# Attention scores of a head pair in one burst, the maxima moved to SBUF, and corner transposes two at a time

## The chip, the cores and the metric

The kernel runs on one core of one Trainium2 chip. The time is the device time of one execution, in microseconds (us); lower is better. The kernel before took 3621.35 us, the median of 3 runs (3619.87 to 3623.71). PE is TensorE, DVE is VectorE, ACT is ScalarE, POOL is GpSimd; SP issues the DMAs here.

## The reference, cut to what matters

The input x has 16 sequences of 256 tokens and 128 channels. It is normalised, and the result goes through a selective scan (the first 330 us or so of the kernel, not touched by the change) and through a stack of six layers of local attention and a gated feed-forward part; the two are multiplied at the end. The change is in the attention:

```
for i in range(DEPTH):                                   # 6
    x = attn_layer(shift_tokens(x), Wqkv[i], ...) + x
    x = ffn_layer(shift_tokens(x), ln_g[i], ...) + x

# attn_layer: 16 heads of 64, windows of 32
qkv = x @ Wqkv;  q, k = l2norm and rotary of q, k
sim = einsum('bhwie,bhwje->bhwij', bq, bk2) * QK_SCALE   # a query sees its own window and the one before
sim = where(mask, -max, sim);  attn = softmax(sim)
out = einsum('bhwij,bhwje->bhwie', attn, bv2);  return out @ Wo
```

## The kernel before, in words

The 4096 tokens are 8 groups of two sequences (512 columns). One group in one layer is an item; there are 48. `flow` runs `turn` once per item on every engine, and the turns of four items overlap: `turn` has the roles prev2, prev, cur and nxt. A turn has 16 steps, and a step is one (head pair p, sequence b) with p = s // 2 and b = s % 2. All order is written out by hand; the engines are tied by semaphores alone. A wait of an engine holds up all that is behind it on that engine.

In step s of a turn PE does, in this order: `scores(s)` (line 844, eight 64x64 matmul tiles of 96 columns for head pair p and sequence b, the two heads of the pair into banks 0 and 1); what `bank_work` gives for "dn", "wo", "rqT" and "cen" together with `down` and `project_out` (lines 911, 883, 789, 889); on even steps `outputs` (line 872, 16 products of probabilities and values); `transpose_probs` of three steps ago (lines 853 and 854, into bank 2); on odd steps a piece of v (lines 355 to 357 with 256 columns); then `bank_work` for "qk", the feed-forward products and the variance (lines 355 to 357 with 512 columns, and 893), and every fourth step `square_sums` (line 826).

DVE does `denominators` (a reciprocal, line 1633), `copy_probs` (line 1639 transposes two 32x32 corners in SBUF, line 1640 copies bank 2), `products` (two rotary products of qk block s - 1, line 1608), and `maxima(s)`: four masked copies of the scores with a running maximum (line 1653, each followed by the read of its accumulator), and one multiplication of the four maxima by the scale of the head (line 1659, `nb`). The four maxima, `mx`, lie in four columns of bank 1 in PSUM. `scores(s)` waits for `sc_bias` of step s - 1, which line 1659 sets, since both use the same columns of banks 0 and 1. ACT then takes the exponentials (`probabilities`, line 1181), and copies v and the outputs out of bank 3 (lines 1195 and 1190). POOL normalises the probabilities (line 1343, after the reciprocal), adds the halves of the rotary product (`rotate`, line 1357, after a DMA has swapped partitions) and scales k (`scale_k`, line 1363, in some steps); in steps 10 to 13 it also has the layer norm and the low parts (lines 1373, 1375, 1386, 1381).

Of the kernel before, what the change touches and what calls it, by code (L numbers as in the profile page):

```python
# [123 lines left out]
SCORE_TILES = [(0, 0, 0), (1, 32, 32), (2, P, P - WINDOW), (3, P + 64, P + 32)]  # L124
# [11 lines left out]
def build(nc, x_in, W_in, W_xdbl, W_dt, W_out, mvec, Wqkv, Wo, W1, W2, lvec, tabs_c, mask_c, ident_c,  # L136
          headsum_c, conv_w, out):
    ctx = ExitStack()
    with ctx:
        def sb(name, shape, dt=F32):  # L140
            return ctx.enter_context(nc.sbuf_tensor(name, shape, dt))
# [48 lines left out]
        nb = sb("nb", [P, STEPS, 2, 2])  # L190
        den = sb("den", [P, STEPS, 2, 2])
# [13 lines left out]
        mx = bank[1][:, UW:UW + 4].rearrange("p (t i) -> p t i", t=2)  # L205
# [142 lines left out]
        def head_scale(t, p, b):  # L348

            m = p % 4 // 2  # L350
            return t[:, p // 4, 2 * b:2 * b + 2, p % 2, 2 * m:2 * m + 2]
# [240 lines left out]
        def _(pe):  # L592
# [167 lines left out]
            def turn(n, o, par, gs, kind, l):  # L760
# [70 lines left out]
                def scores(s):  # L831

                    p, b = s // 2, s % 2
                    scaled = (n8 + (p + 1))
                    used = (n16 + s)
                    if b == 0:
                        pe.wait_ge(k_norm, scaled)
                    pe.wait_ge(sc_bias, used)
                    c0 = b * SEQ
                    for half, c, k0 in SCORE_TILES:  # L840
                        part = slice(64 * (half % 2), 64 * (half % 2) + 64)
                        for i in range(2):
                            rows = slice(64 * i, 64 * i + 64)
                            mm = pe.matmul(bank[i][part, c:c + 96], rot[rows, p, c0 + 64 * half:c0 + 64 * half + 64],  # L844
                                           rot[rows, PAIRS + p, c0 + k0:c0 + k0 + 96], start=True, stop=True)
                    mm.then_inc(sc_ps, 1)
# [107 lines left out]
                for s in range(16):  # L954
# [5 lines left out]
                    if cur is not None:  # L960
                        scores(s)
# [9 lines left out]
                    if s % 2 == 0 and s < 6 and prev is not None:  # L971
                        outputs(s, s // 2 + 5, prev)
                    if s % 2 == 0 and s >= 6 and cur is not None:
                        outputs(s, s // 2 - 3, cur)
# [447 lines left out]
        def _(dve):  # L1422
# [164 lines left out]
            def turn(n, o, par, gs, kind, l):  # L1587
# [47 lines left out]
                def copy_probs(e, q):  # L1635
# [3 lines left out]
                    dve.transpose(pt[96:128, e % 4, :, 0, P:P + WINDOW], pr[0:32, e % 4, :, 1, 0:WINDOW])  # L1639
# [3 lines left out]
                def maxima(s):  # L1643

                    p, b = s // 2, s % 2
                    scores = (n16 + (s + 1))
                    used = (n16 + (s - 1 if s >= 2 or prev is not None else 0))
                    dve.wait_ge(sc_ps, scores)
# [165 lines left out]
```

## Time and profile before

| what | value |
|---|---|
| runs | 3619.87, 3621.35, 3623.71 us; median 3621.35 us |
| profiled execution: its own time, its span | it is given by its span alone: 3621.6 us, 95570 instructions |
| PE | 3397.7 us busy, 94% |
| DVE | 3201.4 us busy, 88% |
| ACT | 3008.5 us busy, 83% |
| POOL | 2872.2 us busy, 79% |
| granted clock of PE | 0.9 to 1.0 of full speed in every slice |

How to read it: the share of busy time is a mean, and matmuls are pipelined with modelled ends, so that 94% of PE is not PE at its peak. The chain of waits tells which engine was the last to arrive at each place. In the rows further down, a row of the timeline is: start in us, duration in us, engine, line, operation, written tile and read tiles, their shapes, how many, and in brackets the idle time before it and what ended it. A row of the chain is: start, length on the chain, and what it was.

### The profile page before, as it was taken

What the parts mean: (1) busy time and instruction counts of PE and PEld (TensorE: products, weight loads), DVE (VectorE), ACT (ScalarE), POOL (GpSimd) and SP (SyncE); (2) the same over time, 40 slices, a digit from 0 to 9 for tenths busy, and PEclk for the clock granted to TensorE, in tenths of its full rate; (3) what the DMA queues carried; (4) which work ended last, traced back from release to release, by engine and by line L of the source; (5) the groups of instructions that cost most, each with busy time, mean ns of one, the idle gap of its engine ahead of it and who ended that gap; (6) DMA issues with size and microseconds to landing.
All of it is one profiled execution on the core that took longest, in us unless ns stands there. A gap on an engine that the chain in (4) does not pass through costs nothing.

```text
span 3621.6 us, 95570 instructions
## 1 busy us (share of the span) xinstructions
PE 3397.7 (94%) x30862; PEld 2172.1 (60%) x30862; DVE 3201.4 (88%) x11640; ACT 3008.5 (83%) x8812; POOL 2872.2 (79%) x2383
## 2 busy tenths in 40 slices
PE   7887999999999999999999999999999999999998
PEld 3444666666666666666666666666666666666665
DVE  6997988988888988998988988988988988998997
ACT  6554888888888888888888888888888888888887
POOL 6887887887887887887788887888787788887783
PEclk9998999999999999999999999999999999999999
DMA  5443322333322333323332332333332333332322
GB/s 160 141 133 121 111 101 101 107 113 106 112 102 100 106 115 103 116 101 100 107 115 103 113 106 96 109 118 102 114 103 98 104 120 105 111 106 98 104 103 92
DMA packets 261741, 396.41 MB, mean 109 GB/s; under 512 B 45566, under 2 KB 86588, under 8 KB 261244
## 3 DMA queue, kind: packets, MB, share of 16 engines
q1 hardware_dynamic: 261244, 390.30, 32.1%
q8 instruction: 249, 4.08, 0.5%
q14 instruction: 248, 2.03, 0.2%
HBM read 157.91 MB, written 6.03 MB: 45 GB/s over the span
## 4 chain that ended last, share of the span: by engine, by line
PE 51%; DVE 22%; POOL 10%; issue 9%; ACT 6%; DMA 1%; SPq 1%; DVEq 0%; POOLq 0%; ACTq 0%
PE bank L883 8%; DVE ab L1608 6%; PE bank L872 6%; PE bank L844 5%; PE bank L355 5%; PE bank L357 5%; PE bank L356 5%; PE bank L826 4%; DVE sm L1653 4%; PE bank L911 4%; PE bank L853 3%; POOL rot L1357 3%; DVE wide L1500 3%; POOL pr L1343 3%; PE bank L854 2%
## 5 line engine op out<-in xcount | busy, mean ns | idle before, releaser
L1181 ACT ACTIVATE pr<-sm,nb,rq 128x128 f32<-128x128 f32 (+1 forms) x3072 | 1517.4, 501 | 16.4 <-DVE nb L1659 16.0
L1343 POOL TENSOR_TENSOR pr<-pr,rden 128x640 f32<-128x640 f32 x768 | 963.6, 1255 | 494.6 <-DVE rden L1633 493.6
L1608 DVE TENSOR_TENSOR ab<-bank,ltab 128x512 f32<-128x512 f32 x1520 | 974.3, 683 | 78.9 <-PE bank L357 64.9
L1357 POOL TENSOR_TENSOR rot<-ab,swp 128x512 f32<-128x512 f32 x760 | 974.6, 1282 | 83.2 <-DMA swp<-ab 82.2
L1653 DVE CUSTOM_DVE_ANT_0 sm<-bank,mask 128x128 f32<-128x128 f32 (+1 forms) x3072 | 841.0, 330 | 43.2 <-PE bank L844 42.4
L1181 ACT ACTIVATION_READ_ACCUMULATOR pr<-sm,nb,rq 128x1 f32 x3072 | 596.6, 194 | 0.0
L844 PEld LDWEIGHTS bank<-rot 64*64 64x64 f32 x12288 | 288.3, 132 | 440.2 <-issue 341.2
L1640 DVE COPY pt<-bank 128x512 f32<-128x512 f32 x768 | 531.4, 692 | 10.2
L1363 POOL TENSOR_TENSOR rot<-rot,rkb 128x512 f32<-128x512 f32 x384 | 490.3, 1282 | 52.6 <-DMA rkb<-k_scratch 51.9
L1169 ACT ACTIVATE sq<-bank 128x512 f32<-128x512 f32 x768 | 452.4, 589 | 62.4 <-DVE ab L1608 49.5
L844 PE MATMUL bank<-rot 64*64 64x96 f32 x12288 | 432.1, 256 | 64.0 <-POOL rot L1363 34.1
L872 PEld LDWEIGHTS bank<-pt,vtok 128*64 128x64 f32 x6144 | 369.2, 137 | 197.7 <-issue 144.2
L872 PE MATMUL bank<-pt,vtok 128*64 128x160 f32 (+1 forms) x6144 | 462.2, 293 | 27.1 <-ACT vtok L1195 27.1
L1653 DVE DVE_READ_ACCUMULATOR2_ANT bank<- 128x1 f32 x3072 | 437.2, 142 | 0.0
L853 PE MATMUL bank<-ident,pr 128*128 128x128 f32 x1536 | 409.1, 293 | 17.8 <-DVE pt L1640 17.5
L1195 ACT ACTIVATE vtok<-bank 128x512 f32<-128x512 f32 x384 | 228.0, 594 | 220.2 <-PE bank L357 220.2
L854 PE MATMUL bank<-ident,pr 128*128 128x128 f32 x1536 | 377.6, 273 | 0.0
L883 PE MATMUL bank<-wide,wo 128*128 128x512 f32 x768 | 370.9, 606 | 0.0
L1190 ACT ACTIVATE wide<-bank 128x512 f32<-128x512 f32 x384 | 227.6, 593 | 156.7 <-PE bank L872 156.2
L355 PE MATMUL bank<-xh,wqk_h 128*128 128x512 f32 x768 | 335.6, 437 | 10.3 <-ACT sq L1169 7.0
L1639 DVE STREAM_TRANSPOSE pt<-pr 32x64 f32<-32x64 f32 x768 | 183.1, 238 | 158.2 <-PE bank L854 137.9
L357 PE MATMUL bank<-xl,wqk_h 128*128 128x512 f32 x768 | 305.5, 398 | 0.0
(213 smaller groups left out, 6160.6 us busy)
## 6 DMA issues: line engine op xcount, KB each, us to landing
swp<-ab SPq DMA_DIRECT2D x1520, 128.0 KB, 2.0
rkb<-k_scratch SPq DMA_DIRECT2D x768, 128.0 KB, 2.9
rot<-c_scratch SPq DMA_DIRECT2D x64, 256.0 KB, 3.3
sq<-c_scratch SPq DMA_DIRECT2D x64, 256.0 KB, 3.2
xs<-xT SPq DMA_DIRECT2D x95, 128.0 KB, 2.3
xs<-xT SPq DMA_DIRECT2D x95, 127.5 KB, 2.4
raw<-Wqkv SPq DMA_DIRECT2D x48, 128.0 KB, 2.5
wo<-Wo SPq DMA_DIRECT2D x6, 512.0 KB, 4.8
```

The source lines that it names most:

```text
L355: eng.matmul(o, wh, ah, start=True, stop=False)
L844: mm = pe.matmul(bank[i][part, c:c + 96], rot[rows, p, c0 + 64 * half:c0 + 64 * half + 64], rot[rows, PAIRS + p, c0 + k0:c0 + k0 + 96], st ...
L853: pe.transpose(bank[2][:, 256 * i:256 * i + P], pr[:, e % 4, i, 0, 0:P], ident[:, :])
L872: mm = pe.matmul(bank[3][64 * i:64 * i + 64, cols], vtok[:, 2 * b + t, ch], pt[:, e % 4, i, t, 0:cols.stop - cols.start], start=(b == 0 an ...
L883: mm = pe.matmul(use_bank("wo", 0)[:, :], wo[:, p, :], wide[:, p, :], start=(p == 0), stop=(p == PAIRS - 1))
L1181: ins = act.activation(pr[:, s % 4, i, t, 0:P + WINDOW * t], sm[:, s % 2, i, cs], ACT.Exp, bias=nb[:, s, t, i:i + 1], scale=head_scale(rq, ...
L1343: ins = pool.tensor_tensor(pr[:, e % 4, :, :, :], pr[:, e % 4, :, :, :], rden[:, e, :, :].rearrange("p t i -> p i t").unsqueeze(3) .to_bro ...
L1357: pool.tensor_tensor(rot[:, PAIRS * (j % 2) + j // 2, :], ab_of(j, 0, lead), swp_of(j, lead), ALU.add).then_inc(qk_rot, 1)
L1363: pool.tensor_tensor(rot[:, PAIRS + p, :], rot[:, PAIRS + p, :], rkb[:, p % KSLOT, :], ALU.mult)\
L1608: ins = dve.tensor_tensor(seqs(ab_of(j, i, lead)), seqs(qk_bank(j, lead)[:, :]), ltab[:, 2 * (j % 2) + i:2 * (j % 2) + i + 1, :] .to_broad ...
L1640: dve.tensor_copy(pt[:, e % 4, :, :, 0:P], bank[2][:, :].rearrange("p (i t c) -> p i t c", i=2, t=2)).then_inc(p_Tsb, 1)
L1653: ins = dve.tensor_tensor_reduce(sm[:, s % 2, i, cs], bank[i][:, cs], mask[:, cs], 1.0, -3e38, ALU.add, ALU.max, mx[:, t, i:i + 1])
```

## The change

Six things change. (1) PE's `scores` runs on even steps only and does both sequences of the head pair in one burst of 16 tiles; it waits for `nb` of the two steps before, once. (2) In banks 0 and 1 the scores of the two sequences now lie side by side (256 columns each), at the column of their key; the first tile has 64 columns in place of 96. DVE's `maxima` reads them there, and waits for the burst, which on odd steps has long been there. (3) With the banks full, `mx` moves from bank 1 to an SBUF tile, one set of four for each sequence. (4) PE's `outputs` stands right behind the scores, ahead of "dn", "wo", "rqT" and "cen". (5) `copy_probs` transposes the corners of steps e and e + 1 in one instruction at even e, and none at odd e; that one also waits for POOL's `p_norm` of e + 1. (6) Semaphore counts follow.

```diff
-SCORE_TILES = [(0, 0, 0), (1, 32, 32), (2, P, P - WINDOW), (3, P + 64, P + 32)]
+SCORE_TILES = [(0, 64), (32, 96), (P - WINDOW, 96), (P + 32, 96)]
+        mx = sb("mx", [P, 2, 2, 2])
-        mx = bank[1][:, UW:UW + 4].rearrange("p (t i) -> p t i", t=2)
@@ PE
-                def scores(s):
-                    p, b = s // 2, s % 2
-                    scaled = (n8 + (p + 1))
-                    used = (n16 + s)
-                    if b == 0:
-                        pe.wait_ge(k_norm, scaled)
-                    pe.wait_ge(sc_bias, used)
-                    c0 = b * SEQ
-                    for half, c, k0 in SCORE_TILES:
-                        part = slice(64 * (half % 2), 64 * (half % 2) + 64)
-                        for i in range(2):
-                            rows = slice(64 * i, 64 * i + 64)
-                            mm = pe.matmul(bank[i][part, c:c + 96], rot[rows, p, c0 + 64 * half:c0 + 64 * half + 64],
-                                           rot[rows, PAIRS + p, c0 + k0:c0 + k0 + 96], start=True, stop=True)
+                def scores(p):
+                    pe.wait_ge(k_norm, n8 + (p + 1))
+                    pe.wait_ge(sc_bias, n16 + 2 * p)
+                    for b in range(GB):
+                        c0 = b * SEQ
+                        for m, (k0, count) in enumerate(SCORE_TILES):
+                            part = slice(64 * (m % 2), 64 * (m % 2) + 64)
+                            for i in range(2):
+                                rows = slice(64 * i, 64 * i + 64)
+                                mm = pe.matmul(bank[i][part, c0 + k0:c0 + k0 + count],
+                                               rot[rows, p, c0 + 64 * m:c0 + 64 * m + 64],
+                                               rot[rows, PAIRS + p, c0 + k0:c0 + k0 + count], start=True, stop=True)
                     mm.then_inc(sc_ps, 1)
...
-                    if cur is not None:
-                        scores(s)
+                    if s % 2 == 0 and cur is not None:
+                        scores(s // 2)
+                    if s % 2 == 0 and s < 6 and prev is not None:
+                        outputs(s, s // 2 + 5, prev)
+                    if s % 2 == 0 and s >= 6 and cur is not None:
+                        outputs(s, s // 2 - 3, cur)
                     bank_work(s, ("dn", "wo", "rqT", "cen"))
...
-                    if s % 2 == 0 and s < 6 and prev is not None:
-                        outputs(s, s // 2 + 5, prev)
-                    if s % 2 == 0 and s >= 6 and cur is not None:
-                        outputs(s, s // 2 - 3, cur)
@@ DVE
-                    dve.transpose(pt[96:128, e % 4, :, 0, P:P + WINDOW], pr[0:32, e % 4, :, 1, 0:WINDOW])
+                    if e % 2 == 0:
+                        both = slice(e % 4, e % 4 + 2)
+                        dve.wait_ge(p_norm, n16 + (16 * q + e + 2))
+                        dve.transpose(pt[96:128, both, :, 0, P:P + WINDOW], pr[0:32, both, :, 1, 0:WINDOW])
...
-                    dve.wait_ge(sc_ps, scores)
+                    dve.wait_ge(sc_ps, n8 + (p + 1))
...
-                            ins = dve.tensor_tensor_reduce(sm[:, s % 2, i, cs], bank[i][:, cs], mask[:, cs],
-                                                           1.0, -3e38, ALU.add, ALU.max, mx[:, t, i:i + 1])
+                            keys = slice(b * SEQ, b * SEQ + P) if t == 0 else slice(b * SEQ + P - WINDOW, b * SEQ + SEQ)
+                            ins = dve.tensor_tensor_reduce(sm[:, s % 2, i, cs], bank[i][:, keys], mask[:, cs],
+                                                           1.0, -3e38, ALU.add, ALU.max, mx[:, b, t, i:i + 1])
...
-                    dve.tensor_tensor(nb[:, s, :, :], mx, head_scale(nrq, p, b), ALU.mult).then_inc(sc_bias, 1)
+                    dve.tensor_tensor(nb[:, s, :, :], mx[:, b, :, :], head_scale(nrq, p, b), ALU.mult).then_inc(sc_bias, 1)
```

PE at steps 0 and 1 of a turn, before: `rot` are the rotated q and k (scores), `gg,w` is the down product, `pt,vtok` the outputs, `ident,pr` the transposes.

```order
L844 MATMUL bank<-rot 64x96 x8
L911 MATMUL bank<-gg,w 128x512
L872 MATMUL bank<-pt,vtok 64x160 x2
L872 MATMUL bank<-pt,vtok 64x128 x2
L872 MATMUL bank<-pt,vtok 64x160 x2
L872 MATMUL bank<-pt,vtok 64x128 x2
L853 MATMUL bank<-ident,pr 128x128
...
L826 MATMUL bank<-sq,headsum 32x512 x4
L844 MATMUL bank<-rot 64x96 x8
L911 MATMUL bank<-gg,w 128x512
L853 MATMUL bank<-ident,pr 128x128
```

The same place of PE in the changed kernel:

```order
L841 MATMUL bank<-rot 64x64 x2
L841 MATMUL bank<-rot 64x96 x6
L841 MATMUL bank<-rot 64x64 x2
L841 MATMUL bank<-rot 64x96 x6
L870 MATMUL bank<-pt,vtok 64x160 x2
L870 MATMUL bank<-pt,vtok 64x128 x2
L870 MATMUL bank<-pt,vtok 64x160 x2
L870 MATMUL bank<-pt,vtok 64x128 x2
L909 MATMUL bank<-gg,w 128x512
...
L826 MATMUL bank<-sq,headsum 32x512 x4
L909 MATMUL bank<-gg,w 128x512
L851 MATMUL bank<-ident,pr 128x128
```

The second burst has joined the first, and the outputs have moved ahead of the down product.

DVE at the end of a step and the start of the next, before (every step reads so); `mask` rows are the maxima, `ISA bank 128x1` the read of an accumulator, and the waits are in brackets:

```order
L1653 ISA sm,bank<-bank,mask 128x160
L1653 ISA bank 128x1
L1659 TENSOR_TENSOR nb<-bank,nrq 128x4 [waits sc_max]
L1633 RECIPROCAL rden<-den 128x4 [waits p_exp]
L1639 STREAM_TRANSPOSE pt<-pr 32x2x32 [waits o_ps,p_T]
L1640 COPY pt<-bank 128x4x128
L1608 TENSOR_TENSOR ab<-bank,ltab 128x512 [waits qk_rot,qk_proj]
```

DVE in the changed kernel, at the start of an even step and then of an odd one:

```order
L1654 ISA mx 128x1
L1660 TENSOR_TENSOR nb<-mx,nrq 128x4 [waits sc_max]
L1631 RECIPROCAL rden<-den 128x4 [waits p_exp]
L1640 STREAM_TRANSPOSE pt<-pr 32x4x32 [waits p_norm,o_ps,p_T]
L1641 COPY pt<-bank 128x4x128
...
L1654 ISA mx 128x1
L1660 TENSOR_TENSOR nb<-mx,nrq 128x4 [waits sc_max]
L1631 RECIPROCAL rden<-den 128x4 [waits p_exp]
L1641 COPY pt<-bank 128x4x128 [waits o_ps,p_T]
```

One transpose in two steps is gone, and both inputs of the multiplication that makes `nb` now lie in SBUF, where one of them lay in PSUM.

## Rows read from the trace of the kernel before

**Rows 1.** The page, parts 1 and 4: busy time, and the chain by engine.

```profile
PE 3397.7 (94%) x30862; PEld 2172.1 (60%) x30862; DVE 3201.4 (88%) x11640; ACT 3008.5 (83%) x8812; POOL 2872.2 (79%) x2383
PE 51%; DVE 22%; POOL 10%; issue 9%; ACT 6%; DMA 1%; SPq 1%; DVEq 0%; POOLq 0%; ACTq 0%
```

**Rows 2.** The chain, 1500 to 1640 us: start, length, what.

```profile
1522.99 1.06 PE bank L889 x2
...
1561.05 0.49 PE bank L844 x16
1561.54 1.06 PE bank L911 x2
...
1564.94 1.91 PE bank L883 x4
1566.86 1.13 PE bank L872 x16
1567.99 0.26 PE bank L853
...
1570.82 1.72 PE bank L883 x4
1572.54 0.11 PE bank L853
...
1584.36 1.13 PE bank L872 x16
...
1590.76 1.06 PE bank L889 x2
```

**Rows 3.** Timeline of PE inside one burst of scores.

```profile
2011.31 0.31 PE L844 MATMUL bank<-rot 64*64 64x96 f32 x4
...
2011.31 0.56 PE L844 MATMUL bank<-rot 64*64 64x96 f32 x16
```

**Rows 4.** Timeline of DVE and ACT from step 5 to step 9 of a turn.

```profile
1578.96 0.24 DVE L1639 STREAM_TRANSPOSE pt<-pr 32x64 f32<-32x64 f32 x1 [1.68 <-PE bank L854]
...
1586.34 0.16 DVE L1659 TENSOR_TENSOR nb<-bank,nrq 128x4 f32<-128x4 f32 x1
...
1586.62 0.24 DVE L1639 STREAM_TRANSPOSE pt<-pr 32x64 f32<-32x64 f32 x1
1586.87 0.69 DVE L1640 COPY pt<-bank 128x512 f32<-128x512 f32 x1
...
1589.87 0.16 DVE L1659 TENSOR_TENSOR nb<-bank,nrq 128x4 f32<-128x4 f32 x1
...
1592.06 0.58 ACT L1255 ACTIVATE gg<-bank 128x512 f32<-128x512 f32 x1
...
1596.15 0.69 DVE L1666 TENSOR_SCALAR rsum<-bank 128x512 f32<-128x512 f32 x1 [0.33 <-PE bank L826]
```

**Rows 5.** The page, part 5: the rotary products on DVE.

```profile
L1608 DVE TENSOR_TENSOR ab<-bank,ltab 128x512 f32<-128x512 f32 x1520 | 974.3, 683 | 78.9 <-PE bank L357 64.9
```

**Rows 6.** Line 1448 of the prologue: its eight instructions, durations in ns.

```profile
L1448 DVE TENSOR_TENSOR rsum<-rsum x8: 135/136/734, 7.4 to 215.2; 128x4 f32<-128x4 f32 x8
```

**Rows 7.** Timeline of DVE and POOL around two of these eight.

```profile
40.74 1.27 POOL L1310 TENSOR_TENSOR wide<-wide,rot 128x512 f32<-128x512 f32 x1
41.29 0.73 DVE L1448 TENSOR_TENSOR rsum<-rsum 128x4 f32<-128x4 f32 x1
...
111.82 0.14 DVE L1448 TENSOR_TENSOR rsum<-rsum 128x4 f32<-128x4 f32 x1
111.98 1.27 POOL L1310 TENSOR_TENSOR wide<-wide,sq 128x512 f32<-128x512 f32 x1 [1.31 <-DVE wide L1500]
```

**Rows 8.** Timeline of POOL and DVE, steps 7 and 14 of the same turn.

```profile
1589.61 1.29 POOL L1363 TENSOR_TENSOR rot<-rot,rkb 128x512 f32<-128x512 f32 x1
...
1615.65 1.30 POOL L1357 TENSOR_TENSOR rot<-ab,swp 128x512 f32<-128x512 f32 x1
...
1615.84 0.16 DVE L1659 TENSOR_TENSOR nb<-bank,nrq 128x4 f32<-128x4 f32 x1
```

More of the change, by code:

```diff
@@ L1645, in maxima @@
                     p, b = s // 2, s % 2
-                    scores = (n16 + (s + 1))
                     used = (n16 + (s - 1 if s >= 2 or prev is not None else 0))
-                    dve.wait_ge(sc_ps, scores)
+                    dve.wait_ge(sc_ps, n8 + (p + 1))
                     dve.wait_ge(p_exp, used)
```

## The prediction, made before the changed kernel was run

> **What bounds the kernel now.** I read the page first, then the chain of waits over two items, then the timelines of DVE, PE and POOL in the stretches that the chain names. On the page two engines are nearly full, and the chain goes through PE for half of the span and through DVE for a fifth [rows 1]; so the question is where each of the two is last. The chain answers it. The centring product of step 8 starts at 1522.99 and again at 1590.76: an item takes 67.77 us [rows 2], and 48 of them make 3253 of the 3621.6 us. Inside an item there are two stretches. The PE stretch runs from the feed-forward products of step 14 to the transposes of step 4: every piece of the chain there is a PE piece behind a PE piece (1561.05 to 1572.54 show a part) [rows 2]. The DVE stretch begins at step 5, where DVE waits 1.68 us for those transposes, and then has no idle time from 1578.96 until step 9, where it waits 0.33 us for the square sums at 1596.15 [rows 4]; behind that it goes on without idle time to the rotary products of step 14, whose square lets ACT load the table of gelu, on which the next PE stretch waits. PE and DVE are close to each other at step 8, but a gain on PE between steps 5 and 13 buys nothing by itself.
>
> The page's execution has a span of 3621.6 us and the median of the runs is 3621.35 us, so the sum is made against the span and carries over as it is.
>
> **PE, bursts.** On the chain a burst costs 0.49 us, and then the first full-array product behind it costs more than without it: two passes of the down product take 1.06 us behind a burst, and four of the output projection 1.91 against 1.72; the first transpose 0.26 behind a tiled product and 0.11 behind a full one [rows 2]. So an odd step without its burst saves 0.49 + about 0.17 = 0.66 us. The even step's burst doubles: four passes end 0.31 us after its start and sixteen 0.56 [rows 3], which is 0.083 for two tiles of 96 columns; eight tiles more are 0.33, and two pairs of 64 columns in place of 96 give back 0.028 each, so +0.27. Had the longer burst the full price again it would be +0.49; I keep 0.27, since nothing new starts inside it. A pair of steps saves 0.39.
>
> **PE, outputs ahead of the rest.** They cost 1.13 both behind a full product (1566.86) and right behind scores (1584.36) [rows 2]. One pass between tiled and full array goes away on steps 0, 2, 4 and 8: 0.15 each (0.26 less 0.11). What they wait for is there already: the copy of bank 2 that they need precedes, on DVE, the `nb` for which the scores have just waited.
>
> **The sum of the PE stretch.** Three bursts go (steps 15, 1, 3): 3 x 0.66 = 1.98. Three grow: 3 x 0.27 = 0.81. Three reorderings: 0.45. Gain 1.6 us an item. DVE stays ahead of it here: it works 3.5 us a step [rows 4], where the mean step of an item is 67.77 / 16 = 4.2 and the steps of this stretch are longer than the mean.
>
> **DVE, corners.** Today a step of DVE is 3.53 us from one `nb` to the next (1586.34 to 1589.87), of which the corner transpose takes 0.25 (1586.62 to 1586.87) [rows 4]. An odd step loses these 0.25. On an even step 64 columns become 128: at the slope of the rotary product, 683 ns for 512 columns [rows 5], that is +0.085; bounds are 0 and +0.24. In steps 5 to 14, up to the products of step 14: 5 x 0.25 - 5 x 0.08 = 0.85. About 0.15 is lost again at step 9, since PE reaches the square sums for which DVE waits only behind the scores, outputs, centring and variance of step 8, 0.12 later than now. 0.7 stays. The added wait for `p_norm` of e + 1 costs nothing: POOL's normalisation begins right behind the reciprocal of the step before and takes 1.3 us, while the transpose comes 3.5 us later; queued behind it are the copy of bank 2 and all of the step.
>
> **DVE, `mx` in SBUF.** This is the part with a price that the diff doesn't show. `nb` becomes a product of two SBUF inputs. No instruction of the layers is one now, but the prologue has one of the same size: line 1448, 128 x 4 elements, both inputs and output in SBUF. Of its eight, the median takes 136 ns and one 734 [rows 6]. The one of 734 ns starts at 41.29 while a POOL product is under way (40.74 to 42.01) and ends at 42.02 with it; one of 136 starts at 111.82, when POOL idles [rows 7]. So it waits for the POOL instruction under way, and frees itself about 0.11 us before what the subtraction says (0.60 us late at a remainder of 0.72).
>
> The Trainium skill, "SBUF — State Buffer", section "Who interferes with whom", says that a DVE instruction with two SBUF inputs contends with a GpSimd instruction that reads SBUF, because its second input comes through the shared read interface, and that one with a single SBUF input does not. By that rule `nb` starts to wait, and the maxima, the reciprocal and the corners do not; all POOL instructions here read SBUF. The trace agrees in the one case that it has. Without the rule and that case the sum would be that of the first rival, 3532 us.
>
> How often: I laid every `nb` of the trace beside POOL's instruction under way. In the turn of rows 8, seven of the ten `nb` of steps 5 to 14 fall into one; the first of these is at step 7, 1589.87 in 1589.61 to 1590.90, 1.03 us before its end, the last at step 14, 1615.84 in 1615.65 to 1616.95, 1.11 [rows 4, 8]. Over all 48 items steps 5 to 13, those that lie ahead of the products of step 14, have 4.2 us of such remainders an item (step 12 and 13 0.85 and 0.94 each, step 7 0.69, steps 5, 6 and 8 hardly any); the PE stretch has 0.9, of which PE sees nothing. With 0.11 off each of some seven hits that is 3.4. That is the upper end if nothing moves. But each wait leaves DVE just behind an end of POOL's, and POOL (79% busy) itself waits for DVE's reciprocal, so the hits thin out. Stepping through the turn of rows 4 and 8 with DVE steps of 3.29 and 3.61 us, I find waits at steps 7, 9, 10, 11 and 13 and none at 8 and 12. The lower end is the average of steps 12 and 13 and a trifle, 1.9. I take 2.9, nearer to the row-by-row reading than to that, less the 0.7 of the corners: the DVE stretch gets 2.2 us longer an item. The accumulator reads that now write SBUF, four a step at 142 ns, are taken at no change; nothing shows them either way, and 10 ns each would be 0.3 us an item.
>
> **Sum.** 2.2 - 1.6 = +0.6 us an item; of 48 items the first and the last have half of each: 47 x 0.6 = 28 us. 3621.6 + 28 = 3650 us.
>
> **Rivals.**
> - *The small product doesn't wait.* For: seven of the eight of line 1448 took 136 ns. Against: at those seven POOL was idle. Then the gain of the PE stretch, 1.6, and of DVE's corners in steps 5 to 8, 0.4, stand; ACT gives back 0.1: it copies the centred sums right after its exponentials (at 1592.06 [rows 4]), these come 1.4 us later now that burst and outputs are in front, and its copy of v is then late for the outputs of step 10. 1.9 x 47 = 89 us: 3532 us.
> - *The hits don't thin out, and the PE stretch feels them too.* For: POOL has more work than DVE in steps 9 to 13, so an `nb` there nearly always finds it busy. Loss 3.4 in the DVE stretch less 0.7, plus 0.3 where `nb` of step 1 or 3 now holds up the next burst, against a gain of 1.2 where the burst has its full price: +1.8 x 47 = 85 us, 3706 us, and 3735 where POOL's weight splits come on top.
> - *The waits are absorbed.* They come to 1.9, a loss of 1.2 in the DVE stretch net of the corners; gain 1.6: -0.4 x 47 = -19 us, 3603 us; it decides at a wait of 2.3 us an item, where the gain of 1.6 and the 0.7 are used up. Below that the kernel is faster than before: this is the other side of the forecast.
> - *It doesn't save the switches*: the 0.17 behind a burst belongs to whatever comes first in a step. Then the three odd steps save 0.49 only and the gain is 1.1: +1.1 x 47 = 52 us, 3673 us; it lies in the forecast's own range.
>
> **How the numbers follow.** Forecast with the last rival, 3625 to 3690: 0.47. Full hits, 3690 to 3740: 0.13. Absorbed, 3560 to 3625: 0.25. No wait, about 3532: 0.15. A measurement of this kernel tells a change of 0.2%, 7 us, from none: 3614 to 3629. About 0.05 of the forecast and 0.04 of the absorbed case lie there, so faster 0.36, same 0.09, slower 0.55. The range that leaves out the no-wait case and the ends of the others is 3550 to 3725; the forecast's own is 3625 to 3690.
>
> **What would show it.** `nb` should grow from 162 ns to a mean of 300 to 500, with single ones up to 1.3 us, and each long one should end with a POOL instruction; if it stays near 150 ns, the first rival holds. The matmul bursts should be 384 with about 0.76 us on the chain, followed by outputs at 1.13, and the odd steps should start with a transpose of 0.11 or a projection at 1.72 for four. The corners should be 384 of 0.3 us. The item should take about 68.4 us, DVE's share of the chain should rise and PE's fall below 50%. The prediction is wrong in its larger part if the item stays under 67.4 us.

## The result, and the profile after

| kernel | median, us | lowest to highest | runs |
|---|---|---|---|
| before | 3621.35 | 3619.74 to 3623.71 | 5 |
| after | 3633.72 | 3631.35 to 3637.96 | 5 |

The changed kernel takes 1.0034 of the time before, 95% interval [1.0023, 1.0045]: 12.4 us slower, where +28 was forecast.

The page of the changed kernel, parts 1 and 4, against [rows 1]:

```profile
span 3632.4 us, 95188 instructions
...
PE 3315.3 (91%) x30862; PEld 2180.4 (60%) x30862; DVE 3202.3 (88%) x11256; ACT 3016.2 (83%) x8812; POOL 2882.2 (79%) x2383
...
PE 44%; DVE 25%; ACT 16%; issue 10%; POOL 4%; DMA 1%; DVEq 0%; SPq 0%; ACTq 0%; POOLq 0%
```

PE is busy for 82 us less, and its products of the scores (lines 844 and 841) for 88 us less: 343.6 in place of 432.1. DVE is as busy as before, though half of the corner transposes are gone. ACT's share of the chain went from 6 to 16%: nothing in the forecast spoke of that. The clock has no part in the difference: its mean over the span is 0.995 of full speed in both kernels. (The table before the change says 0.9 or more for every slice; in both kernels the fourth of the 40 slices, around the end of the scan, shows 0.8 to 0.9.)

DVE's groups that the change touches, before and then after: line, engine, operation, written and read tile, shapes, count, then busy us and mean ns of one, then idle time before them.

```profile
L1653 DVE CUSTOM_DVE_ANT_0 sm<-bank,mask 128x128 f32<-128x128 f32 (+1 forms) x3072 | 841.0, 330 | 43.2 <-PE bank L844 42.4
...
L1653 DVE DVE_READ_ACCUMULATOR2_ANT bank<- 128x1 f32 x3072 | 437.2, 142 | 0.0
...
L1639 DVE STREAM_TRANSPOSE pt<-pr 32x64 f32<-32x64 f32 x768 | 183.1, 238 | 158.2 <-PE bank L854 137.9 <-issue 0.6
...
L1659 DVE TENSOR_TENSOR nb<-bank,nrq 128x4 f32<-128x4 f32 x768 | 124.5, 162 | 26.2
```

```profile
L1654 DVE CUSTOM_DVE_ANT_0 sm<-bank,mask 128x128 f32<-128x128 f32 (+1 forms) x3072 | 753.6, 301 | 4.3 <-PE bank L841 4.2
...
L1660 DVE TENSOR_TENSOR nb<-mx,nrq 128x4 f32<-128x4 f32 x768 | 332.8, 433 | 26.6
...
L1654 DVE DVE_READ_ACCUMULATOR2_ANT mx<- 128x1 f32 x3072 | 253.8, 83 | 0.0
...
L1640 DVE STREAM_TRANSPOSE pt<-pr 32x128 f32<-32x128 f32 x384 | 116.9, 304 | 13.7 <-PE bank L852 1.5 <-issue 0.3
```

`nb` grew from 162 to 433 ns, inside the 300 to 500 that was asked for. The corners are 384 of 304 ns, as priced. But the reads of the accumulator fell from 142 to 83 ns and the masked copies from 330 to 301, which was priced at nothing. Part of a copy's record lies under its read; by their starts in the timelines the four copies and reads of a step take 1.02 us where they took 1.20.

Timeline of DVE and POOL in the changed kernel, two `nb` with the POOL instructions that run beside them:

```profile
1592.44 1.27 POOL L1355 TENSOR_TENSOR rot<-ab,swp 128x512 f32<-128x512 f32 x1
...
1593.38 0.35 DVE L1660 TENSOR_TENSOR nb<-mx,nrq 128x4 f32<-128x4 f32 x1
...
1601.32 1.28 POOL L1371 TENSOR_TENSOR gg<-gg 128x512 f32<-128x512 f32 x1
...
1601.97 0.65 DVE L1660 TENSOR_TENSOR nb<-mx,nrq 128x4 f32<-128x4 f32 x1
```

The first ends at 1593.73, POOL's rotation at 1593.71; the second ends at 1602.62 and POOL's product at 1602.60. So it is in the whole trace: 406 of the 768 `nb` take more than 0.22 us, and each of them ends within 0.03 us of the end of a POOL instruction. The wait is the one forecast from line 1448 [rows 6, 7].

The chain of the changed kernel, from the table of gelu to step 3, which answers to [rows 2]:

```profile
1553.72 0.60 ACT wide L1188
1554.32 1.61 ACT pr L1179 x7
...
1556.28 0.49 ACT sq L1167
1556.81 0.50 PE bank L355
...
1557.78 0.82 PE bank L841 x29
1558.60 1.13 PE bank L870 x16
...
1561.92 1.00 PE bank L826 x8
1562.91 1.06 PE bank L909 x2
...
1567.77 1.91 PE bank L881 x4
...
1570.82 0.86 PE bank L909 x2
1571.68 1.72 PE bank L881 x4
```

Three things are to be seen. A double burst costs 0.82 us, 0.33 more than the single one and not 0.27 (some of its 32 records are missing). At step 3 the switch is saved in full: the down product takes 0.86 and four passes of the projection 1.72. At step 1 it isn't: the down product still takes 1.06, now behind the square sums of line 826. And the chain enters the PE stretch through ACT: block 15 of q and k (line 355 at 1556.81) starts only when ACT has squared block 14, which stands behind all exponentials of step 14.

The waits that the change made or took away; the first fence is the kernel before, the second the changed one. Who waited, for whom, us in total, times, longest.

```profile
ACT wide L1190 <- PE bank L872: 156.2, 137, 1.6
...
PEld bank L355 <- ACT sq L1169: 42.9, 141, 2.1
...
ACT pr L1181 <- DVE nb L1659: 16.0, 52, 5.0
...
DVE rsum L1666 <- PE bank L826: 15.5, 46, 0.4
...
PE bank L355 <- ACT sq L1169: 7.0, 6, 1.9
...
DVE rq L1617 <- PE bank L789: 1.3, 2, 0.8
```

```profile
ACT pr L1179 <- DVE nb L1660: 156.6, 195, 6.0
...
PEld bank L355 <- ACT sq L1167: 71.3, 129, 4.0
...
DVE rq L1615 <- PE bank L789: 61.0, 48, 2.2
...
ACT gg L1253 <- PE bank L887: 53.9, 47, 1.2
...
DVE rsum L1667 <- PE bank L826: 40.7, 47, 0.9
...
PE bank L355 <- ACT sq L1167: 23.4, 59, 3.8
```

ACT no longer waits for the outputs. In exchange DVE waits for the product rqT, ACT for the centring product (both stand behind the outputs now), PE longer for ACT's square, and ACT longer for `nb`.

To place the time I took the end of each of the 768 `nb` and summed the time from one to the next over two parts of the item, as means of items 3 to 46, in us. The same was done for the runs of the next section:

| kernel | steps 6 to 13 | steps 14 to 5 | item |
|---|---|---|---|
| before | 30.48 | 37.71 | 68.19 |
| after | 31.49 | 36.90 | 68.39 |
| b1, before with `mx` in SBUF | 32.15 | 37.57 | 69.72 |
| b3, the same with the lock taken away | 30.19 | 37.53 | 67.72 |
| a1, after with the lock taken away | 29.98 | 36.84 | 66.82 |
| a2, after with rqT and cen first | 31.06 | 37.04 | 68.10 |
| e1, a2 with the square moved | 31.00 | 36.55 | 67.55 |

So DVE's stretch lost 1.0 and PE's won 0.8. "The lock" below is `nb`'s wait for POOL's instruction. In a1, b3, c2, d3 and f1 `nb` is made from four columns of scores in place of the maxima, so that one input is in PSUM; the maxima are made and written all the same, but `nb` leaves them out, and so these five kernels do not compute the reference.

### The profile page after: what moved, and what is told of

Same layout as the page of the kernel before. It is cut to its first block, busy times and chain, and to the rows that moved or that the text cites. A ratio compares the mean times of both kernels' runs of the same rounds, so it can differ in the third digit from the quotient of the medians.

```text
span 3632.4 us, 95188 instructions
## 1 busy us (share of the span) xinstructions
PE 3315.3 (91%) x30862; PEld 2180.4 (60%) x30862; DVE 3202.3 (88%) x11256; ACT 3016.2 (83%) x8812; POOL 2882.2 (79%) x2383
## 4 chain that ended last, share of the span: by engine, by line
PE 44%; DVE 25%; ACT 16%; issue 10%; POOL 4%; DMA 1%; DVEq 0%; SPq 0%; ACTq 0%; POOLq 0%
PE bank L881 8%; DVE ab L1606 8%; PE bank L870 7%; ACT pr L1179 6%; DVE sm L1654 6%; PE bank L841 5%; PE bank L909 4%; PE bank L355 4%; PE bank L357 3%; PE bank L356 3%; DVE wide L1498 3%; DVE pt L1641 3%; PE bank L826 2%; PE bank L851 2%; PE bank L852 2%
## 5 line engine op out<-in xcount | busy, mean ns | idle before, releaser
L1606 DVE TENSOR_TENSOR ab<-bank,ltab 128x512 f32<-128x512 f32 x1520 | 974.9, 683 | 43.8 <-PE bank L357 35.9
L1654 DVE CUSTOM_DVE_ANT_0 sm<-bank,mask 128x128 f32<-128x128 f32 (+1 forms) x3072 | 753.6, 301 | 4.3 <-PE bank L841 4.2
L1641 DVE COPY pt<-bank 128x512 f32<-128x512 f32 x768 | 525.4, 684 | 95.3 <-PE bank L852 86.8
L1167 ACT ACTIVATE sq<-bank 128x512 f32<-128x512 f32 x768 | 454.9, 592 | 86.7 <-DVE ab L1606 79.6
L870 PE MATMUL bank<-pt,vtok 128*64 128x160 f32 (+1 forms) x6144 | 461.4, 292 | 41.0 <-ACT vtok L1193 38.8
L851 PE MATMUL bank<-ident,pr 128*128 128x128 f32 x1536 | 399.2, 287 | 38.3 <-DVE pt L1641 38.3
L841 PE MATMUL bank<-rot 64*64 64x96 f32 (+1 forms) x12288 | 343.6, 243 | 86.7 <-DVE nb L1660 77.1
L841 PEld LDWEIGHTS bank<-rot 64*64 64x64 f32 x12288 | 275.7, 133 | 233.6 <-issue 147.7
L851 PEld LDWEIGHTS bank<-ident,pr 128*128 128x128 f32 x1536 | 215.0, 140 | 299.3 <-issue 254.9
L852 PE MATMUL bank<-ident,pr 128*128 128x128 f32 x1536 | 377.8, 273 | 0.0
L1660 DVE TENSOR_TENSOR nb<-mx,nrq 128x4 f32<-128x4 f32 x768 | 332.8, 433 | 26.6
L356 PE MATMUL bank<-xh,wqk_l 128*128 128x512 f32 x768 | 302.7, 394 | 0.0
```

The costliest lines, as they stand in the source:

```text
L841: mm = pe.matmul(bank[i][part, c0 + k0:c0 + k0 + count], rot[rows, p, c0 + 64 * m:c0 + 64 * m + 64], rot[rows, PAIRS + p, c0 + k0:c0 + k0 ...
L851: pe.transpose(bank[2][:, 256 * i:256 * i + P], pr[:, e % 4, i, 0, 0:P], ident[:, :])
L870: mm = pe.matmul(bank[3][64 * i:64 * i + 64, cols], vtok[:, 2 * b + t, ch], pt[:, e % 4, i, t, 0:cols.stop - cols.start], start=(b == 0 an ...
L1606: ins = dve.tensor_tensor(seqs(ab_of(j, i, lead)), seqs(qk_bank(j, lead)[:, :]), ltab[:, 2 * (j % 2) + i:2 * (j % 2) + i + 1, :] .to_broad ...
L1641: dve.tensor_copy(pt[:, e % 4, :, :, 0:P], bank[2][:, :].rearrange("p (i t c) -> p i t c", i=2, t=2)).then_inc(p_Tsb, 1)
L1654: ins = dve.tensor_tensor_reduce(sm[:, s % 2, i, cs], bank[i][:, keys], mask[:, cs], 1.0, -3e38, ALU.add, ALU.max, mx[:, b, t, i:i + 1])
```

## The experiments

Each ran beside the kernel before, whose median was 3620.42 to 3623.37 us there; ratios are against it, with 95% intervals.

| run | median, us | ratio |
|---|---|---|
| a1_psum_operand | 3553.36 | 0.9815 [0.9801, 0.9828] |
| b1_mx_sbuf | 3689.15 | 1.0187 [1.0173, 1.0201] |
| b3_mx_sbuf_psum_operand | 3598.33 | 0.9938 [0.9924, 0.9952] |
| b2_corners_pair | 3607.40 | 0.9965 [0.9952, 0.9977] |
| a3_outputs_old | 3627.33 | 1.0019 [1.0010, 1.0028] |
| a2_rq_cen_first | 3616.59 | 0.9988 [0.9979, 0.9997] |
| c1_four_scalars | 3642.53 | 1.0058 [1.0045, 1.0070] |
| c2_psum_rq_cen | 3547.83 | 0.9797 [0.9783, 0.9810] |
| f1_psum_single | 3564.08 | 0.9838 [0.9825, 0.9852] |
| d1_nb_on_pool | 3717.76 | 1.0264 [1.0250, 1.0278] |
| d2_nb_pool_square | 3700.06 | 1.0217 [1.0199, 1.0234] |
| d3_psum_square | 3525.34 | 0.9732 [0.9719, 0.9746] |
| e1_a2_square | 3593.53 | 0.9921 [0.9907, 0.9934] |
| e3_before_square | 3619.38 | 0.9992 [0.9983, 1.0001] |
| e2_b2_square | 3605.99 | 0.9958 [0.9945, 0.9972] |

**a1, the changed kernel without the lock.**

```diff
-dve.tensor_tensor(nb[:, s, :, :], mx[:, b, :, :], head_scale(nrq, p, b), ALU.mult).then_inc(sc_bias, 1)
+near = bank[1][:, 0:4].rearrange("p (t i) -> p t i", t=2)
+dve.tensor_tensor(nb[:, s, :, :], near, head_scale(nrq, p, b), ALU.is_lt).then_inc(sc_bias, 1)
```

> The changed kernel, but the product that makes nb reads four columns of bank 1 (PSUM) in place of mx and only compares them with the scale, so the maxima are not used and its output is not the reference's; instructions, counts and waits are the same, mx is still written to SBUF. Theory (the port wait): nb falls from a mean of 433 ns to about 165, no long ones are left, the stretch of DVE from step 5 to 13 loses its 3.2 us of waits an item; since PE and ACT are close behind, some 2 to 2.5 us of it reach the item: 3633.7 - 47 x 2.25 = about 3528 us (3515 to 3545). Rival (the waits are hidden behind ACT or PE, and the small gain of the change is all that there is): 3615 us or more.

Measured: 3553.36 us, 80 less than the changed kernel, where 89 to 119 less were expected. The chain on its page, and the group of `nb`:

```profile
PE 48%; ACT 32%; DVE 7%; issue 6%; POOL 5%; DMA 1%; SPq 0%; DVEq 0%; ACTq 0%; POOLq 0%
...
L1661 DVE TENSOR_TENSOR nb<-bank,nrq 128x4 f32<-128x4 f32 x768 | 124.1, 162 | 26.7
```

`nb` is back at 162 ns, with the same size and the same tiles around it. The lock is shown, and its price here: without it the change would be faster than before. But it costs 80 us for 3.15 us of waits an item (what the `nb` of steps 5 to 13 take over 0.15 us each), which would be 148 over 47 items. The rest was hidden behind other waits of DVE, which come out when the lock is taken away:

```profile
DVE pt L1641 <- PE bank L852: 139.6, 236, 2.4
DVE ab L1606 <- PE bank L357: 97.7, 220, 1.9
...
DVE rden L1631 <- ACT pr L1179: 75.3, 100, 1.3
```

In the changed kernel these three were 86.8, 35.9 and 43.0 us; together they grow by 147 us. The chain says who is next: ACT has 32% of it.

**b1 and b3, the lock and the reads in the kernel before.** b1 moves `mx` to SBUF and does nothing else; b3 adds a1's edit to b1.

```diff
+        mx = sb("mx", [P, 2, 2])
-        mx = bank[1][:, UW:UW + 4].rearrange("p (t i) -> p t i", t=2)
...
```

> The kernel before with mx in an SBUF tile and nothing else changed. Both theories expect accumulator reads of 83 ns in place of 142 and 1.02 us in place of 1.20 from the first maximum to nb, and nb at 350 to 500 ns. Theory (waits outweigh the faster reads): nine steps save 0.18 each = 1.6 us, waits of about 3.2 us come, so +1.6 x 47 = 75 us, less what moves behind PE: 3650 to 3700 us. Rival (the faster reads pay for the waits, the loss of the change comes from its other parts): 3610 to 3635 us.

> The kernel before with mx written to SBUF, but nb made by a comparison of four columns of bank 1 (PSUM) with the scale, so that the maxima are not used in it. It has the faster accumulator reads without the port wait. If the wait is what costs in b1 (3689 us) and the reads are a gain of their own: nine steps of the DVE stretch x 0.18 = 1.6 us an item, less what becomes a wait for PE there: 3621 - 45 to 76 = 3545 to 3576 us. If the reads give nothing on the path: 3615 to 3625 us.

Measured: b1 3689.15, within what was expected; b3 3598.33, where 3545 to 3576 was. The lock costs 91 us in the kernel before, and the shorter reads and copies by themselves bring 22. They save 0.17 us a step (step 7 went from 3.53 to 3.36), 1.4 over the eight steps, but the stretch gets only 0.29 shorter: step 9 grows from 4.56 to 4.89 and step 11 from 3.91 to 4.06. DVE's waits say why; b3:

```profile
DVE pt L1639 <- PE bank L854: 200.8, 293, 2.5
DVE ab L1608 <- PE bank L357: 83.8, 183, 2.2
...
DVE rden L1633 <- ACT pr L1181: 22.9, 56, 0.9
```

The three were 137.9, 64.9 and 7.0 us before. A faster DVE waits for PE's transposes and ACT's exponentials.

**b2, the paired corners in the kernel before**, and **f1, c2 with single corners.** b2 has part 5 of the change alone.

> The kernel before with the corner transposes of two steps as one (part 5 alone). The prediction had 5 x 0.25 - 5 x 0.08 = 0.85 us of DVE in the stretch from step 5 to 14, 0.7 of it on the path: 3621 - 33 = 3588 us (3580 to 3600). Rival (DVE's time there is not the item's, or the new wait for p_norm takes it back): 3615 to 3625 us.

> Kernel c2 with a corner transpose in every step, as before: it has bursts, outputs and the faster reads, without the paired corners and without the port wait. If DVE still sets the stretch, undoing 0.85 us of it costs up to 40 us: 3570 to 3588. If ACT now runs next to DVE there (the chain of c2 goes through ACT from step 9 to 14), it costs as little as in the kernel before or less: 3550 to 3563 us. Against the kernel before with faster reads alone (3598) it also says what bursts and outputs are worth: predicted 1.6 us an item, 75 us.

Measured: b2 3607.40, 13 less than the 3620.42 beside it, where 0.7 x 47 = 33 was priced; f1 3564.08, which is 16 more than c2. So the pairing is worth 13 to 16 us in either kernel. f1 against b3 is what bursts and outputs (with rqT and cen first) bring: 34 us where the forecast had 1.6 x 47 = 75.

**a3 and a2, where the outputs stand.** a3 puts them back where they were, behind all four; a2 leaves them but puts rqT and cen ahead. The edit of a2:

```diff
+                    bank_work(s, ("rqT", "cen"))
                     if s % 2 == 0 and s < 6 and prev is not None:
                         outputs(s, s // 2 + 5, prev)
                     if s % 2 == 0 and s >= 6 and cur is not None:
                         outputs(s, s // 2 - 3, cur)
-                    bank_work(s, ("dn", "wo", "rqT", "cen"))
+                    bank_work(s, ("dn", "wo"))
```

> The changed kernel with the outputs in their old place behind all of dn, wo, rqT and cen (part 4 of the change undone). If moving the outputs gains only its 0.15 us on three steps of the PE stretch: 0.45 x 47 = +21 us, 3655 us. If its cost (q norms and centring late) outweighs that: 3600 to 3630 us. If a2 is right about rqT and cen alone, this one lies 15 to 25 us above a2.

> The changed kernel with the transposes of the q norms (step 4) and the centring product (step 8) ahead of the outputs again, as before; the down and output projections stay behind them. Theory (outputs ahead of these two cost what they gain): the wait of DVE for the q norms (61 us in all) and of ACT for the centred sums (54 us) go; they reach the item by half: 3633.7 - 50 = about 3585 us (3570 to 3615). Rival (these waits are off the path, since DVE and ACT have slack at steps 4 and 8): 3628 to 3640 us.

Measured: a3 3627.33, 6 less than the changed kernel, a2 3616.59, 17 less, where some 50 were expected. a2 and a3 differ only in whether the outputs stand ahead of the down product and the projection, so that this half of the move is worth 11 us, where 0.45 x 47 = 21 was forecast. In a2 the waits for rqT are down to

```profile
DVE rq L1616 <- PE bank L789: 2.4, 2, 1.2
```

from 61.0, and that of ACT for the centring product is gone. The 1.27 us an item at step 4 did not come back there, though: step 4 fell from 5.97 to 4.81 and step 5 rose from 4.00 to 5.24, where DVE now waits for the transposes instead. What a2 won, 0.43 us, it won in steps 6 to 13, mostly in step 11 (3.73 to 3.36) and step 12 (4.06 to 3.82); it lost 0.14 in the rest. Whether that comes from the earlier centring product or from fewer locks in those steps (2.7 us an item in steps 5 to 13, where the changed kernel has 3.15) is not separated.

**c1, a2 with `nb` as four instructions of one column**, each with a single SBUF tensor and a scale read through a pointer.

```diff
-dve.tensor_tensor(nb[:, s, :, :], mx[:, b, :, :], head_scale(nrq, p, b), ALU.mult).then_inc(sc_bias, 1)
+rate = head_scale(nrq, p, b)
+for t in range(2):
+    for i in range(2):
+        ins = dve.tensor_scalar(nb[:, s, t, i:i + 1], mx[:, b, t, i:i + 1], rate[:, t, i:i + 1], None, ALU.mult)
+ins.then_inc(sc_bias, 1)
```

> Kernel a2 (q norms and centring ahead of the outputs) with nb made by four products of one column by a pointer scalar each, mx in SBUF. Theory: an instruction with one SBUF tensor input of one element doesn't wait for POOL, so the long ones go; three more small instructions a step add about 0.25 us, nine of them 2.25 us an item in place of 3.2 us of waits: 3616.6 - 0.9 x 47 = 3575 us (3560 to 3600). Rival (each of the four still waits for POOL, as line 1443 of the prologue does with one tensor and a constant): 3640 us or more.

Measured: 3642.53, 26 more than a2, where 42 less were expected. Its group of `nb`:

```profile
L1664 DVE TENSOR_SCALAR nb<-mx,nrq 128x1 f32<-128x1 f32 x3072 | 443.0, 206 | 27.4
```

Four take 0.58 us (443.0 over 768 steps), where one under the lock takes 0.43 on the mean. No one of the 3072 takes over 0.22 us, so the lock is avoided. The time is where the rival had it, but not for its reason: the price of three more instructions is above that of the lock. Against a2 the item is 0.5 us longer, 0.33 of it in steps 14 to 5, where the lock costs next to nothing.

**d1 and d2, `nb` on POOL** (whole reference, on top of a2): POOL multiplies at the end of its step, behind its other work, and the burst waits for the maxima alone. d2 also moves ACT's square of step 14 ahead of the exponentials.

> Kernel a2 with the product that makes nb on POOL, as the last instruction of POOL's step, and the burst of scores waiting for the maxima (sc_max) in place of nb; all of the reference is computed. DVE then has no instruction with two SBUF tensor inputs in the layers. If the port wait on DVE is the cost, its removal gives what a1 and c2 gave, less what 768 small products cost POOL and the exponentials that now wait for POOL's queue in steps 10 to 14: between c2 (3548) and a2 (3617), near 3565 us. If a late nb is what costs, wherever it waits, the exponentials wait for POOL as long as before and it stays at 3610 us or more.

> Kernel d1 with ACT's square of block 14 ahead of the exponentials of step 14 (behind the gelu). If PE's block 15 waits there for ACT, which the chain of the changed kernel shows (copy, exponentials, square, then L355): 0.5 to 1 us an item, 25 to 45 us below d1. If the exponentials of step 14 are then what is late: within 8 us of d1.

Measured: d1 3717.76, 101 more than a2, where some 50 less were expected; d2 3700.06. d1's waits, and then its group of `nb`:

```profile
POOL nb L1352 <- DVE mx L1664: 368.0, 292, 4.5
ACT pr L1180 <- POOL nb L1352: 260.6, 268, 6.0
DVE rden L1641 <- ACT pr L1180: 226.7, 266, 2.0
```

```profile
L1352 POOL TENSOR_TENSOR nb<-mx,nrq 128x4 f32<-128x4 f32 x768 | 156.5, 204 | 368.5 <-DVE mx L1664 368.0
```

The product takes POOL 204 ns, at most 242, and shows no lock. But POOL then stands waiting for the maxima with its next normalisation behind it, ACT for POOL, and DVE's reciprocal for ACT: a ring of three engines, in some 270 to 290 of the 768 steps. DVE falls to 78% busy and the kernel is slower still.

**c2 and d3, how far it goes without the lock.** c2 is a1 with a2's edit, d3 is c2 with the square moved:

```diff
+                    if nxt is not None and s == 14:
+                        square(s, nxt)
                     if cur is not None:
                         probabilities(s)
...
-                        square(s, nxt)
+                        if s != 14:
+                            square(s, nxt)
```

> Kernels a1 and a2 together: nb reads bank 1 and leaves the maxima out, q norms and centring stand ahead of the outputs. If the two causes are independent: 3553.4 - 17 = 3536 us. If the late q norms and centring cost only while DVE is held by the port: 3550 to 3556 us.

> Kernel c2 (nb from bank 1, maxima not used; q norms and centring first) with the same square of block 14 ahead of the exponentials: 3547.8 - 25 to 45 = 3503 to 3523 us if the missing gain of PE lies in that wait for ACT; within 8 us of 3548 if not.

Measured: c2 3547.83, d3 3525.34. rqT and cen first bring 6 us here, where they brought 17 with the lock: neither the 3536 of independent causes nor the 3550 or more of the other reading. The chain of c2 from step 9 on, through the gelu to block 15 of q and k:

```profile
2032.54 0.63 ACT rsum L1201
...
2038.19 1.42 ACT pr L1180 x6
...
2041.63 1.97 ACT pr L1180 x8
...
2055.55 1.61 ACT pr L1180 x7
...
2057.51 0.49 ACT sq L1168
...
2058.04 0.50 PE bank L355
```

Without the lock the DVE stretch is ACT's from step 9 on, and it ends with the square for which PE waits. Moving that square brings 22 us here and 18 between d1 and d2; the 25 to 45 that were expected of both are too much.

**e1, e3 and e2: the square in the changed kernel and in the one before.** These three settle where the rest of PE's gain was, with the whole reference computed: e1 is a2, e3 the kernel before and e2 b2, each with d3's edit.

> The changed kernel with rqT and the centring product ahead of the outputs, and ACT's square of step 14 ahead of the exponentials of step 14; it computes the whole reference. Theory (part of the gain that PE should have had lies in its wait for that square before block 15 of q and k, 71.3 + 23.4 us in the changed kernel): the 18 and 22 us of the two earlier pairs come here too, 3616.6 - 18 = 3598 us (3590 to 3607). Rival (the lock on DVE sets the item from end to end, so an engine that is earlier finds nobody waiting): within 7 us of 3616.6.

> The kernel before with the move of the square alone. Theory (it is the shorter and earlier PE stretch of the changed kernel that makes ACT last there): before, that wait has 42.9 + 7.0 = 49.9 us against 94.7 in the changed kernel, so the move should bring at most half as much, some 9 us: 3612 us. Rival (the square stands in the wrong place whatever PE does): 18 to 22 us here too, 3601 us. A second rival: nothing, since ACT has the exponentials then later for the transposes: 3621.

> The kernel before with the paired corner transposes and the move of the square. Theory: b2's 3607.4 less what the move brings in the kernel before, some 9 us: 3598 us, a little under the changed kernel with both moves, so that bursts with the maxima in SBUF bring nothing over it. Rival: DVE, with fewer corners, leaves PE and ACT last more often, 18 us: 3589 us.

Measured: e1 3593.53, 23 less than a2. e3 3619.38: 3 less than the kernel before beside it, with an interval that holds no change. e2 3605.99, 1.4 less than b2 (3.3 if each is taken against the kernel before beside it), above both of the times expected, 3598 and 3589. So the wait for the square is worth 18 to 23 us in the three kernels tried that have the bursts, and next to nothing in the two that lack them. That it is the bursts, which make PE early, is argued and not shown: all three kernels also have the outputs ahead and `mx` in an SBUF tile, which no run separates from the bursts here. The rival that had it as a fault of either kernel (18 to 22 us) falls, and so do the 9 us that I had read from the sum of its waits; that it brings nothing at all in the kernel before is not excluded. In e1 the waits of PE are

```profile
PEld bank L355 <- ACT sq L1168: 43.2, 82, 3.9
...
PE bank L355 <- ACT sq L1168: 18.4, 28, 3.7
```

(75.3 and 29.3 us in a2), and steps 2 and 3 of the item are 0.30 and 0.25 shorter than in a2. e1 computes all of the reference and beats both kernels: 0.9921 of the time before, [0.9907, 0.9934].

## Why the prediction was off in size

The direction and the mechanism held: `nb` waits for POOL. The price of each part did not. Terms in us an item; the measured ones are differences of the table of stretches, in the order before, b3, a1, after:

| term | forecast | measured |
|---|---|---|
| reads and copies into SBUF | 0 | -0.47 (-0.29 and -0.18) |
| bursts, outputs, corners | -1.6 - 0.7 = -2.3 | -0.90 (-0.21 and -0.69) |
| the lock | +2.9 | +1.57 (+1.51 and +0.06) |
| sum | +0.6 | +0.20 |

- **What bounds the kernel.** I took steps 5 to 14 as DVE's alone and the rest as PE's alone, from a chain that shows only who came last. The step that failed is this one, and the rest follows. With 1.4 us taken off DVE in the stretch, b3 gave 0.29: PE and ACT were that near. With the locks taken off, a1 gave 1.51 of 3.15, since PE and ACT came next.
- **The lock.** The count was right: 3.15 us of waits an item in steps 5 to 13 against 2.9 forecast. The mis-sized term is what they cost, 1.5. About half of them stand where DVE would have waited for PE or ACT anyway. The 1.3 us of waits outside these steps cost 0.06, as said ("of which PE sees nothing"). The rival *absorbed* had the idea but put it on the number of waits ("it decides at a wait of 2.3 us"); what decides is the slack of the next engine. *No wait* is excluded by a1 and b1. *Full hits* had the price of waits as if none were hidden.
- **A rule with an exception.** The prediction says that the trace agrees in the one case that it has, and that an instruction with a single SBUF input does not contend. For two inputs that holds. For one it is too wide: the Trainium skill, "SBUF — State Buffer", section "Who interferes with whom", says it only of instructions outside DVE's two-port modes. And the same prologue has a case against it, line 1443, four columns of one SBUF tensor and a constant. Two of its eight, at which POOL idled, took 170 ns; the six others took 674 to 1204 ns, started while a POOL instruction was under way and ended within 0.04 us of its end. In which mode they ran no run shows. It cost the forecast nothing, since the maxima, the reciprocal and the corners did not wait, but the rule as told there should not be carried over.
- **The reads.** "Taken at no change", with 10 ns each as an example. They fell by 59 ns each and the copies by 29; worth 22 us in b3. The forecast put this term at nothing.
- **PE, bursts.** Three odd bursts at 0.66 and three even ones at +0.27. Measured on the chain: +0.33 for an even one, and at step 1 the switch stays, so that 0.49 is saved there and 0.69 at step 3 (0.49, and the 0.20 between 1.06 and 0.86). The rival *switches not saved* was right for one of the two odd steps that the chain shows. This is 0.17 + 3 x 0.06 = 0.35 us of the missing gain.
- **PE, outputs ahead.** "What they wait for is there already" held but for step 10, where they waited for ACT's copy of v before as well (27.1 us in all, then 38.8). But the forecast did not ask who waits for what they were put ahead of. That was DVE (rqT, 61.0 us) and ACT (cen, 53.9 us). With both moved ahead a2 gives 17 us.
- **PE's stretch.** It entered with the square of step 14 behind exponentials. The forecast said "every piece of the chain there is a PE piece", true of the kernel before, where ACT was just ahead. In the changed kernel ACT was behind, and e1 against e3 shows 23 against 3 us. After a2 and e1 PE's stretch is 1.16 shorter than before, of the 1.6 priced.
- **Corners.** 0.3 us each, 384 of them: right. Of the 33 us 13 came. In b2, which has nothing else, DVE's corners are 66 us shorter in all, and its waits for PE grow: for the transposes from 137.9 to 162.0, for the q and k products from 64.9 to 79.6, for the scores from 42.4 to 50.9, and for the square sums at 1596.15 [rows 4] from 15.5 to 27.9. This last wait is 40.7 in the changed kernel and 27.6 in a3, so that the outputs ahead of the sums make the rest of it.
- **The item.** 68.4 us between the centring products was asked for; in the same place of the changed kernel they stand at 1524.05 and 1592.34, 68.29. But the forecast built this on one item of 67.77, and the mean item before was 68.19: that the 68.4 came out is luck. The mean over the items is 0.2 above before, not 0.6. The share of DVE in the chain rose and that of PE fell below 50%, as said.

What stays open: how the 17 us of a2 divide between DVE's and ACT's wait (they were moved together), and whether paired bursts would pay under an `nb` that computes the reference without the lock, since banks 0 and 1 have no free column and neither form tried without it (four columns, POOL) was cheaper; `mx` in a column of another bank was not tried.

## What to carry over

Before a gain or a loss is multiplied by the number of steps, find how far behind the next engine is in that stretch; here every term, gain and loss alike, arrived at about a half or less, mostly because another engine was close behind. When work is moved ahead on one engine, list who waits for each thing it was moved past, and once an engine has become faster, look at the first instruction of its stretch: the move of one ACT instruction brought 3 us, not clear of no change, in the kernel before, and 23 in a2. A small operand moved from PSUM to SBUF changes both the instructions that write it and those that read it, and here the two went opposite ways, by 22 and 91 us.

## What the runs showed of the hardware

- A DVE reduction whose accumulator goes to SBUF is shorter than one whose goes to PSUM: the read 83 ns against 142, the masked copy ahead of it 301 against 330 on the mean, in b1, b3 and the changed kernel alike.
- A DVE product of two SBUF inputs waits for the POOL instruction under way even when it is tiny: one of 128 x 4 elements took 0.65 us because a POOL product had that long to go. Over 768 of them it cost 91 us in the kernel before (b1 against b3) and 80 in the changed one. With one input in PSUM the same instruction took 162 ns on the mean. That is the rule of the Trainium skill, "SBUF — State Buffer", section "Who interferes with whom", for two SBUF inputs; the trace agrees, and the runs add the price.
- Four DVE instructions of one column with a scale through a pointer take 206 ns each as recorded, 0.58 us together, and do not show the wait (the longest is 217 ns). Line 1443, four columns and a constant, also with a single SBUF tensor as input, does: 674 to 1204 ns in six of eight, against 170. The 128 x 4 product takes 204 ns on POOL.
- The dearer first full-array product (1.06 against 0.86 us for two passes) follows the square sums (at 1562.91 in the changed kernel) as it follows a burst of scores (at 1561.54 [rows 2]); behind the outputs four passes take 1.91 us (at 1567.77) where they take 1.72 behind a full-array product (at 1571.68).
